# Attention scores from Q and K over 64 channels, two heads on the two row halves, in place of x A x^T over 128

## What is computed

```python
Q = (x @ Wq.T).reshape(b, n, H, R)      # H = 8, R = 64
K = (x @ Wk.T).reshape(b, n, H, R)
V = (x @ Wv.T).reshape(b, n, H, d)      # d = 128
attn = jnp.einsum('bnhr,bmhr->bhnm', Q, K)
attn = jax.nn.softmax(attn, axis=-1)
out = jnp.einsum('bhnm,bmhd->bnd', attn, V)
x = _layernorm(x + out)
# lin(a, w): einsum('bsi,oi->bso')
h = silu(lin(x, w1) * w1_s) * (lin(x, w2) * w2_s)
h = gelu(lin(h, h1) * h1_s)
h = gelu(lin(h, h2) * h2_s)
x = _layernorm(x + lin(h, w3) * w3_s)
```

## Time and profile before

| | us |
|---|---|
| median of the 3 runs shown | 1096.17 |
| lowest and highest | 1095.11, 1096.27 |
| span of the profiled execution | 1095.1 |
| PE busy | 1051.1 |
| DVE busy | 819.5 |
| ACT busy | 811.4 |
| POOL busy | 602.9 |

### The profile page before, as it was taken

One profiled execution on the slowest core, in us unless ns is written; L12 is line 12 of the kernel. 1 busy time (PEld: TensorE's weight loads), 2 busy tenths in 40 slices (PEclk: granted clock), 3 DMA queues, 4 the chain that ended last, 5 costly groups with the idle time before them and its releaser, 6 DMA issues.

```text
span 1095.1 us, 20804 instructions
## 1 busy us (share of the span) xinstructions
PE 1051.1 (96%) x6598; PEld 932.7 (85%) x6598; DVE 819.5 (75%) x1722; ACT 811.4 (74%) x1948; POOL 602.9 (55%) x603
## 2 busy tenths in 40 slices
PE   7989999999999999999999998999999999999986
PEld 6878898888889879898798988889898888989864
DVE  5888687786868768687686966869687786968654
ACT  5768778787777867778687876878778787877732
POOL 1326457465565645557456564656657465655742
PEclk9999999999999999999999999999999999999987
DMA  6000000000000000000000000000000000000000
GB/s 173 11 10 12 1 21 2 20 12 21 13 11 21 1 22 12 10 21 2 22 12 11 21 11 13 11 20 12 11 21 1 20 12 11 11 11 11 9 3 20
DMA packets 29862, 18.31 MB, mean 17 GB/s; under 512 B 914, under 2 KB 28580, under 8 KB 29732
## 3 DMA queue, kind: packets, MB, share of 16 engines
q1 hardware_dynamic: 29732, 16.53, 5.2%
HBM read 12.33 MB, written 4.19 MB: 15 GB/s over the span
## 4 chain that ended last, share of the span: by engine, by line
PE 68%; DVE 11%; issue 10%; ACT 5%; POOL 5%; DMA 0%; SPq 0%; POOLq 0%; DVEq 0%; ACTq 0%
PE bank L859 13%; PE bank L860 12%; PE bank L778 11%; PE bank L780 11%; PE bank L779 11%; PE bank L785 8%; DVE neg_max L590 3%; ACT prob L441 2%; POOL prob L345 2%; DVE x L632 1%; DVE pt_lo L559 1%; POOL odd_lo L352 1%; POOL rstd L362 1%; ACT L441 1%; DVE t_lo L559 1%
## 5 line engine op out<-in xcount | busy, mean ns | idle before, releaser
L345 POOL TENSOR_TENSOR prob<-prob,inv_total 128x512 f32<-128x512 f32 x256 | 266.6, 1041 | 213.4 <-DVE inv_total L595 211.9
L441 ACT ACTIVATE prob<-bank,neg_max 128x256 f32<-128x256 f32 x512 | 237.7, 473 | 70.8 <-DVE neg_max L590 69.8
L352 POOL TENSOR_TENSOR odd_lo<-act,odd_hi 128x512 fp32r<-128x512 f32 x120 | 155.2, 1293 | 170.2 <-DVE odd_hi L657 117.0
L559 DVE TENSOR_TENSOR pt_lo<-bank,pt_hi 128x512 fp32r<-128x512 f32 x256 | 172.7, 675 | 60.6 <-ACT pt_hi L410 60.3
L590 DVE TENSOR_REDUCE neg_max<-bank 128x2 f32<-128x512 f32 x256 | 174.1, 680 | 11.5 <-PE bank L780 11.2
L410 ACT ACTIVATE pt_hi<-bank 128x512 fp32r<-128x512 f32 x256 | 149.6, 599 | 28.7 <-PE bank L785 26.8
L778 PE MATMUL bank<-pt_hi,v_hi 128*128 128x256 f32 x512 | 165.9, 324 | 0.0
L778 PE MATMUL bank<-xt_hi,t_hi 128*128 128x256 f32 x512 | 150.8, 295 | 14.9 <-issue 10.7
L785 PE MATMUL bank<-ident,prob 128*128 128x128 f32 x1024 | 155.2, 274 | 1.5 <-issue 0.7
L780 PE MATMUL bank<-xt_hi,t_lo 128*128 128x256 f32 x512 | 145.1, 283 | 0.0
L779 PE MATMUL bank<-xt_lo,t_hi 128*128 128x256 f32 x512 | 144.7, 283 | 0.0
(11 more groups left out here) (116 smaller groups left out, 2555.7 us busy)
## 6 DMA issues: line engine op xcount, KB each, us to landing
x_in<-in_L_attn_x SPq DMA_DIRECT2D x16, 256.0 KB, 2.8
res<-in_L_attn_x SPq DMA_DIRECT2D x16, 256.0 KB, 2.7
out_x<-y SPq DMA_DIRECT2D x16, 256.0 KB, 2.3
h_in<-in_L_ffn_h_w SPq DMA_DIRECT2D x2, 1024.0 KB
w_in<-in_L_ffn_w_w SPq DMA_DIRECT2D x3, 256.0 KB
wv_in<-in_L_attn_Wv SPq DMA_DIRECT2D x1, 512.0 KB, 5.9
wq_in<-in_L_attn_Wq SPq DMA_DIRECT2D x1, 256.0 KB, 4.1
wk_in<-in_L_attn_Wk SPq DMA_DIRECT2D x1, 256.0 KB, 5.0
```

What stands on the lines that cost most here:

```text
L345: nc.gpsimd.tensor_tensor(prob[:, j % RING, :, :], prob[:, j % RING, :, :], inv_total[:, j % RING, :].unsqueeze(2).to_broadcast([P, NT, N] ...
L352: nc.gpsimd.tensor_tensor(lo[:, c, :], act_of(f, c), hi[:, c, :].bitcast(F32), ALU.subtract).then_inc(s_lo, 1)
L441: last = nc.scalar.activation(prob[:, j % RING, nt, :], sc[j % 2][:, nt * N:(nt + 1) * N], ACT.Exp, bias=neg_max[:, j % RING, nt:nt + 1], ...
L559: return nc.vector.tensor_tensor(dst, src, hi.bitcast(F32), ALU.subtract)
```

## The change

A is gone. The prologue transposes Wq and Wk and splits them into hi and lo. `project_t` makes, for even h, the tile of Q^T with heads h and h+1 on rows 0 to 63 and 64 to 127, and for odd h the tile of K^T with heads h-1 and h. The number and shape of its matmuls stay. `scores_of_two(i, j)` makes the scores of the units j and j+1: twelve matmuls of 64 rows and 256 columns, alternately on the upper and the lower row half, into `sc[0]` and `sc[1]`. It waits for the exponentials of unit j-1, since it writes both banks. In the steps it is called in odd slots only, for units j+3 and j+4. The lists of ACT, DVE and POOL stay as they are, but for the names in the prologue.

```diff
-        a_hi, a_lo = (sb(f"a_{s}", [P, H, D], F32R) for s in ("hi", "lo"))
+        wq_hi, wq_lo = (sb(f"wq_{s}", [P, H * R], F32R) for s in ("hi", "lo"))
+        wk_hi, wk_lo = (sb(f"wk_{s}", [P, H * R], F32R) for s in ("hi", "lo"))
...
-            wq_in = sb("wq_in", [R, H, D], at=early)
-            wk_in = sb("wk_in", [R, H, D], at=early)
+            wq_in = sb("wq_in", [P, H * R // P, D], at=early)
+            wk_in = sb("wk_in", [P, H * R // P, D], at=early)
...
-        PREP = [(a_hi[:, 0:4, :], a_lo[:, 0:4, :]), (a_hi[:, 4:8, :], a_lo[:, 4:8, :]),
+        PREP = [(wq_hi[:, :], wq_lo[:, :]), (wk_hi[:, :], wk_lo[:, :]),
...
-            sp.dma_start(wq_in[:, :, :], wq.rearrange("(h r) d -> r h d", h=H)).then_inc(s_wqk, 16)
-            sp.dma_start(wk_in[:, :, :], wk.rearrange("(h r) d -> r h d", h=H)).then_inc(s_wqk, 16)
+            sp.dma_start(wq_in[:, :, :], wq.rearrange("(g p) d -> p g d", p=P)).then_inc(s_wqk, 16)
+            sp.dma_start(wk_in[:, :, :], wk.rearrange("(g p) d -> p g d", p=P)).then_inc(s_wqk, 16)
...
             def project_t(i, h):
                 hi, lo = xt_of(i)
-                three(t_bank(i, h)[:, :], a_hi[:, h, :], a_lo[:, h, :], hi[:, :], lo[:, :],
+                w_hi, w_lo = (wq_hi, wq_lo) if h % 2 == 0 else (wk_hi, wk_lo)
+                cols = slice(h // 2 * P, (h // 2 + 1) * P)
+                three(t_bank(i, h)[:, :], w_hi[:, cols], w_lo[:, cols], hi[:, :], lo[:, :],
                       True, True).then_inc(s_t_mm, 1)
...
-            def scores(i, j):
+            def scores_of_two(i, j):
 
                 b, h = j // H, j % H
-                hi, lo = xt_of(i)
                 if j < H:
-                    pe.wait_ge(s_t_lo, count(i, H, h + 1))
-                need(pe, s_exp, count(i, J, j - 1))
+                    pe.wait_ge(s_t_lo, count(i, H, h + 2))
+                need(pe, s_exp, count(i, J, j))
+                m = slice(b * N, (b + 1) * N)
                 for nt in range(NT):
                     q = slice(b * N + nt * P, b * N + (nt + 1) * P)
-                    m = slice(b * N, (b + 1) * N)
-                    last = three(sc[j % 2][:, nt * N:(nt + 1) * N], t_hi[:, h, q], t_lo[:, h, q],
-                                 hi[:, m], lo[:, m], True, True)
-                last.then_inc(s_sc, 1)
+                    ends = []
+                    for term, (left, right) in enumerate(((t_hi, t_hi), (t_hi, t_lo), (t_lo, t_hi))):
+                        for n in range(2):
+                            rows = slice(n * R, (n + 1) * R)
+                            ends.append(mm(sc[n][:, nt * N:(nt + 1) * N], left[rows, h, q], right[rows, h + 1, m],
+                                           start=(term == 0), stop=(term == 2)))
+                ends[-2].then_inc(s_sc, 1)
+                ends[-1].then_inc(s_sc, 1)
...
-            for g in range(2):
-                for h in range(4):
-                    last = mm(PREP_BANK[g][:, h * D:(h + 1) * D], wq_in[:, 4 * g + h, :], wk_in[:, 4 * g + h, :],
-                              start=True, stop=True)
-                last.then_inc(s_prep_mm, 1)
+            turns(PREP_BANK[0], [wq_in[:, g, :] for g in range(H * R // P)], s_prep_mm)
+            turns(PREP_BANK[1], [wk_in[:, g, :] for g in range(H * R // P)], s_prep_mm)
...
-            scores(first, 0)
-            scores(first, 1)
+            scores_of_two(first, 0)
...
-            scores(first, 2)
+            scores_of_two(first, 2)
...
-                    for pair, u in units(i, j, cur, nxt, LEAD):
-                        scores(pair, u)
+                    for pair, u in units(i, j, cur, nxt, LEAD) if j % 2 == 1 else ():
+                        scores_of_two(pair, u)
```

## The result

| | before | changed |
|---|---|---|
| median | 1096.2 us | 1217.4 us (1216.2 to 1217.7) |
| span of the profiled execution | 1095.1 | 1215.8 |
| PE busy | 1051.1 (96%) | 1029.5 (85%) |
| mean granted clock | 0.987 | 0.975 |

The changed kernel takes 1.1103 times as long, with a 95% interval of 1.109 to 1.1117: 121 us more.

The account below looks back on a forecast made before the run. PE, busy 96%, was taken as the bound, with ACT close behind. Waits 138, new score matmuls 102, removed scores -184, unwon 48 and prologue -2 gave +102 on 1095.1, rounded to 1200 us; range 1150 to 1300.

Parts of the forecast that it names:

- The wait for the exponentials of the unit just in front: At odd slots PE's pair of scores needs exponentials one unit later than before; 8.73 us a step, together 138 us.
- S: PE time of one pair's twelve 64-row score matmuls; taken as 0.80 us with halves overlapping, 102 us for 128 pairs.
- the bound of serial loads: Score matmuls: weight loads of both halves go one after another, S = 1.40, 1276 us; little or no overlap, chance 0.33.
- the 0.11: Closest pitch of a load and a matmul, 0.11 us from the transposes; load or transpose itself left open.
- rival 2: PE empties when changing between whole and half rows, 0.16 us each way, 42 us; overlap with emptying, or both, chance 0.08.
- The waits: Idle before odd slots' first score matmuls, priced slot by slot at 1.01 to 1.93 us; 13 and 15 at nothing.
- the unwon part: Even slots' removed scores, 0.72 us each, only lengthen waiting if ACT is behind: 69 us, of which 48 stay unwon.
- The step of the forecast with slots 6 and 8: In slots 6 and 8 ACT is back to back, so PE's saved 0.72 us there is only more waiting.
- Slots 13 and 15 at nothing: No wait for exponentials in these slots, since a layer of matmuls stands on PE in front of each.
- The clock: New waits stay just below bringing half clock: nothing added; one such stretch in each step would cost at most 27 us.
- The prologue: Sixteen matmul records on 64 rows (3.78 us) give way to eight transposes: 1.8 us less, if the copies follow.

Follow-up runs that it names:

- e1: Kernel before with the scores of units j+3 and j+4 called together in odd slots, still x A x^T over 128 rows: 1279.3 us, ratio 1.1661.
- e4: Changed kernel with ScalarE's exponentials ahead of its copies in even slots (not 10, 12) and both row maxima of a pair in the odd slot: 1128.7 us.
- e2: Changed kernel with scores of one unit at a time in every slot, on one row half each: 1163.3 us, ratio 1.0644.
- e9: Kernel of e2 with each score matmul over all 128 rows in place of one half: 1091.3 us, ratio 0.9958.
- e3: Changed kernel with the twelve score matmuls reordered, six on the upper rows, then six on the lower: 1271.4 us, ratio 1.1595.

## Why the prediction was right, point by point

- **Sign, size and mechanism.** 1200 was forecast and 1217 measured, in the range of 1150 to 1300. The wait for the exponentials of the unit just in front was named as the cause; e1 shows it alone and e4 takes most of it away.
- **S.** Taken as 0.80, measured 0.91. The overlap was right against the bound of serial loads (1.40). Two loads fit into each doubled step of 0.12 us, and PEld's rows of that pair are doubled too (548.16 x2, 548.28 x2): the two halves load side by side. Whether the 0.11 is the load on one half or the transpose stays open. The Trainium skill, page "TensorE: Matmul & The Clock Gate", section "LDWEIGHTS (loading the stationary operand)", gives the time of a load by its columns; with loads one after another that is an estimate of 1.36 for S, and the 0.91 measured decides against such a sum. What the same page says in "Part 3: Packing small matmuls", that matmuls on different row groups run at the same time, the trace bears out (x2 in the timeline above).
- **The 0.11 that S missed** is rival 2. I gave an emptying 0.16 us each way as an alternative, with 0.08 chance; it was in fact part of the case that came true, at 0.27 to 0.33 us both ways together (e2, e9). In the changed kernel it shows as 0.11 in S and 0.05 at the transposes, 20 us in all against the 42 of that rival. Its full cost shows only when PE doesn't stand anyway on the way in.
- **The waits.** Forecast by slot (with the unwon part), and measured in a step at full clock: slot 1 1.5 and 1.78; slot 3 1.3 and 1.32; slot 5 2.2 and 1.76; slots 7 and 9 2.3 and 1.58; slot 11 2.1 and 1.20, with 0.63 more in slot 10. In all 186 us forecast on top of the kernel before, and 154 measured, 9 in slot 10 and 14 at the gate: 177. The step of the forecast with slots 6 and 8, where ACT is back to back and the 0.72 isn't won, was right about ACT: from the start of slot 5's scores to the end of its read in slot 6 it took 7.27 us before and takes 7.20 now. It was wrong about PE, which was to reach slot 7 by 0.72 sooner and does so by 0.12 (5.68 us after the start of slot 5's scores in place of 5.80): the rest goes into S and the waits for DVE's gate, which the forecast put at nothing. So the place of the wait was off more than its size.
- **Slots 13 and 15 at nothing.** Right for 13; slot 15 waits 0.49, 7 us in all.
- **The clock.** I added nothing and gave 27 us as a bound. Half-clock time grew by 33 us, worth up to 16, and by the lengths of the steps it cost some 6. One such stretch stands behind a wait of 1.78 us, shorter than the 2.46 in the earlier trace rows.
- **The prologue.** 1.8 us forecast; its projections start 2.8 earlier. 1.0 of that is not from the transposes: the first matmul on wq and wk starts at 6.04 in place of 7.01, released by the transfer in both.

Sum of the errors: S and the transposes 20 too low, gate 14, slot 10 9 and clock 6 left out, against waits for the exponentials that were 32 too dear. They had opposite signs, and the 17 us between 1200 and 1217 are what they leave. The mechanism was right, but that the number came so near is partly luck.

## What to carry to other kernels

Before two pieces of work are put together to fill the array, ask what the pair needs at its start that each one alone didn't: here both banks, and with them the newest result of another engine. Read that price where it can be read already, as the distance between the time at which the engine now starts that work and the time at which the later input is ready, slot by slot; it adds up. If the order of the producing engine's list is what makes it late, change that first: it was worth 106 us of the 121 here, and matmuls on 64 rows should come in long groups, since each visit cost some 0.28 us here.

## What was not expected of the hardware

- Going from 128-row matmuls to 64-row ones and back costs 0.28 us by the difference of e2 and e9 over 256 visits, 0.27 by their steps at full clock, with three steps of 0.21 to 0.22 us where 0.12 is the rule.
- PE overlaps matmuls of the two row halves even if they are not neighbours in its list: by the doubled rows of e3, three of the lower half ran beside three of the upper that stood in front of them.
- A stretch at half clock followed a wait of under 2 us (window 529.2 to 533.2, granted clock 0.66), and the same wait two steps on was followed by none (676.5 to 680.5, 1.00).
- Half clock can last while PE streams: in e2, behind a stand of 2.05 us in front of 427.59, the granted clock is 0.50 from 430 to 444 us, with PE busy all of these 14 us.
